# Tap products as two 32-column matmuls in branch order, put back through DRAM; one warm-up token fewer; an earlier operand load

## The reference

```python
# layer 1: graph convolution over joints, then four branches over time
x = concat([x[:, :h], einsum('bctv,vw->bctw', x[:, h:], A_flat)])
x = concat([x[:, :h] @ A_intra, x[:, h:] @ A_inter])
y = relu(bn(conv1x1(x + x @ An, Wgc)))
b1 = bn(tconv(relu(bn(conv1x1(y, Wb1))), Wt1, dilation=1))   # 5 taps over time, 8 channels
b2 = bn(tconv(relu(bn(conv1x1(y, Wb2))), Wt2, dilation=2))   # 5 taps, 8 channels
b3 = bn(maxpool3(relu(bn(conv1x1(y, Wb3)))))
b4 = bn(conv1x1(y, Wb4))
t = relu(concat([b1, b2, b3, b4]) + res)                     # res is the input x
# layer 2: attention over the 400 tokens of each of 32 batches, on the normed t
q, k, v = three projections to 32 channels
scores = exp(-(|q|^2 + |k|^2 - 2 q.k));  t = t + softmax(scores) @ v
# layer 3: norm, projection, batch norm over all tokens, then a recurrence over the tokens
y_t = sigmoid(wx_t + y_(t-1) @ V.T);  out = t + y
```

## Time and profile before

| | |
|---|---|
| median of 3 runs | 237.83 us (237.70 to 238.28) |
| profiled execution | 237.66 us, span 235.8 us, mean TensorE clock 0.956 |
| busy, share of span | PE 199.2 us (85%), PEld 94.1 (40%), DVE 157.7 (67%), ACT 169.9 (72%), POOL 27.5 (12%) |
| DMA | 26.83 MB, mean 114 GB/s, one queue |
| head, first pair | 0 to 30 us |
| loop | 30 to 88 us; VectorE's `add_x` stands at 45.82, 65.46 and 85.10 |
| attention | to 199 us |
| recurrence | 208.9 to 227 us, then the output stores |

### The profile page before, as it was taken

The page is one execution under the profiler, slowest core; times in us unless marked ns, Lnnn a source line. Parts: engine busy times, 40 slices in busy tenths (PEclk is TensorE's granted clock), DMA queues, the critical chain, the costliest instruction groups (busy, mean ns, idle before and its releaser), DMA issues. The chain is left out here.

```text
span 235.8 us, 3561 instructions
## 1 busy us (share of the span) xinstructions
PE 199.2 (85%) x1110; PEld 94.1 (40%) x1110; DVE 157.7 (67%) x296; ACT 169.9 (72%) x309; POOL 27.5 (12%) x44
## 2 busy tenths in 40 slices
PE   0775998898899797959989999999999998588950
PEld 0552554464465353523333343434343333245630
DVE  0417618965992992399578577777869695595880
ACT  4028179579759959797998999999899984365640
POOL 6000000054024006016100101010101000000000
PEclk9997699999999999997999999999999999889985
DMA  6940020039599709348880716162520000000016
GB/s 173 372 126 0 0 72 1 0 77 348 160 273 285 221 0 308 129 138 296 212 215 0 192 23 190 22 169 47 176 37 0 3 0 0 0 3 0 0 51 233
DMA packets 26883, 26.83 MB, mean 114 GB/s; under 512 B 1550, under 2 KB 25806, under 8 KB 26740
## 3 DMA queue, kind: packets, MB, share of 16 engines
q1 hardware_dynamic: 26868, 26.64, 38.6%
HBM read 14.74 MB, written 11.88 MB: 113 GB/s over the span
## 5 line engine op out<-in xcount | busy, mean ns | idle before, releaser
L474 ACT ACTIVATE arena<-ps 128x800 f32<-128x800 f32 (+1 forms) x56 | 44.5, 796 | 6.5 <-PE ps L980 4.9
L481 ACT ACTIVATE arena<-arena 128x800 f32<-128x800 f32 (+1 forms) x56 | 46.3, 829 | 0.0
L980 PE MATMUL ps<-qa,ka 128*128 128x400 bf16 (+1 forms) x128 | 35.8, 343 | 3.6 <-ACT arena L474 3.6
L980 PE MATMUL ps<-qb,kb 96*128 96x400 bf16 (+1 forms) x128 | 35.7, 341 | 0.0
L702 DVE TENSOR_TENSOR psum<-arena 128x400 f32<-128x400 f32 x32 | 19.6, 612 | 13.5 <-ACT arena L481 13.4
L702 DVE TENSOR_TENSOR psum<-psum,arena 128x400 f32<-128x400 f32 x32 | 19.5, 609 | 7.2 <-ACT arena L481 5.8
L1013 PE MATMUL ps<-arena,vb 128*32 128x400 f32 x192 | 21.0, 513 | 0.8 <-issue 0.8
L905 PE MATMUL ps<-arena,cst 128*128 128x400 f32 x32 | 15.7, 620 | 6.5 <-DVE arena L627 6.5
L980 PEld LDWEIGHTS ps<-qa,ka 128*128 128x128 bf16 (+1 forms) x128 | 10.4, 98 | 26.9 <-ACT arena L474 10.0
L1094 PE MATMUL ps<-yb,cst 128*128 128x160 f32 x76 | 17.2, 335 | 2.2 <-ACT yb L551 1.3
L711 DVE RECIPROCAL arena<-ps 128x400 f32<-128x400 f32 x7 | 18.6, 2651 | 0.0
(11 more groups left out here) (137 smaller groups left out, 357.4 us busy)
## 6 DMA issues: line engine op xcount, KB each, us to landing
dka<-arena SPq DMA_DIRECT2D x16, 200.0 KB, 3.1
dqa<-arena SPq DMA_DIRECT2D x16, 200.0 KB, 3.2
ka<-dka SPq DMA_DIRECT2D x8, 400.0 KB
qa<-dqa SPq DMA_DIRECT2D x8, 400.0 KB
arena<-x_tok SPq DMA_DIRECT2D x4, 400.0 KB
t<-x SPq DMA_DIRECT2D x1, 1600.0 KB, 12.1
dkb<-arena SPq DMA_DIRECT2D x8, 200.0 KB, 3.5
dqb<-arena SPq DMA_DIRECT2D x8, 200.0 KB, 4.6
```

The source lines that it names most:

```text
L474: nc.scalar.activation(prob[par][:, lo:hi, :], ps[:, o:o + hi - lo, 0:N], ACT.Exp, scale=2.0).then_inc(e1_done, 1)
L481: nc.scalar.activation(p, p, ACT.Exp).then_inc(p_ready, 1)
L980: last = mm_(ps[row:row + keys, bank, 0:N], kk[par][0:rows, b, o:o + keys], qq[par][0:rows, b, :], start=first, stop=not first, skip_group ...
```

## The change

The parts, in the order of the program:

1. x goes into `t0` in branch order, by 16 transfers of 8 partitions in place of one of 128.
2. GpSimd reorders the columns of an identity, of the middle-tap matrix and of the tap matrices; the two tap matrices shrink to 32 columns each. TensorE makes from them a centering matrix and two columns with scale and shift in branch order, and VectorE copies both out of PSUM (three copies where there was one).
3. `taps` now does the middle product first, over all 128 columns, and then two products of 32 columns, one per branch, into PSUM partitions 0 to 31 and 32 to 63. VectorE's maximum is moved ahead of its copies for the second branch.
4. `t_relu` writes to `outs` (now also `pre_t`), in branch order; `center` reads it there with the reordered matrix. For the residual the tensor is stored to DRAM (`store_t`, one transfer per pair) and loaded into `t0` in the old order (`load_t`, four transfers per pair). `residual` waits for them.
5. SyncE's queue is written out without loops: `load_t` and `store_t` stand ahead of `store`, and the operands of group 2 are loaded ahead of the last `de` store.
6. The first sweep starts at token 1 in place of token 0 (`SKIP`), and the seed blocks are cut differently.

```diff
-BLOCKS = ((0, 1), (1, 4), (4, 7), (7, 10))
+BLOCKS = ((0, 2), (2, 5), (5, 8), (8, 10))
+SKIP = 1
...
+        dt = nc.dram_tensor("dt", [PAIRS, P, 2 * N], F32, kind="Internal").ap()
...
+        pre_t = outs
...
+            def store_t(i):
+
+                sp.wait_ge(t0_ready, 2 * i + 2)
+                sp.dma_start(dt[i], pre_t[:, 2 * i:2 * i + 2, :].rearrange("p g n -> p (g n)")).then_inc(t_stored, 16)
+
+            def load_t(i):
+
+                sp.wait_ge(t_stored, 16 * i + 16)
+                if i:
+                    sp.wait_ge(t_in, 16 * NB * i)
+                for b in range(NB):
+                    sp.dma_start(t0[C * b:C * b + C, 2 * i:2 * i + 2, :].rearrange("p g n -> p (g n)"),
+                                 dt[i].rearrange("(j b r) n -> b j r n", j=BR, b=NB)[b]).then_inc(t_in, 16)
...
-            sp.dma_start(t0[:, :, :], x.rearrange("g p n -> p g n")).then_inc(x_in, 16)
+            for j in range(BR):
+                for b in range(NB):
+                    o, to = C * b + CB * j, C * j + CB * b
+                    sp.dma_start(t0[to:to + CB, :, :],
+                                 x[:, o:o + CB, :].rearrange("g p n -> p g n")).then_inc(x_in, 16)
...
-            store(0)
-            for par in range(2):
-                load_operands(0, par)
-            with sp.Fori(1, PAIRS) as i:
+            def load_next(i, par):
+
+                sp.wait_ge(s_done, UNITS * (2 * i + par - 1))
+                load_operands(i, par)
+
+            for i in range(PAIRS - 1):
+                if i:
+                    load_t(i - 1)
+                store_t(i)
                 store(i)
-            with sp.Fori(1, PAIRS) as i:
-                for par in range(2):
-                    sp.wait_ge(s_done, UNITS * (2 * i + par - 1))
-                    load_operands(i, par)
+                store_e(i)
+                if i == 0:
+                    for par in range(2):
+                        load_operands(0, par)
+            load_t(PAIRS - 2)
+            store_t(PAIRS - 1)
+            store(PAIRS - 1)
+            load_next(1, 0)
+            store_e(PAIRS - 1)
+            load_next(1, 1)
+            load_t(PAIRS - 1)
+            for i in range(2, PAIRS):
+                for par in range(2):
+                    load_next(i, par)
...
+            def order_by_branch(dst, src):
+
+                nc.gpsimd.tensor_copy(dst[:, :].rearrange("p (j b r) -> p j b r", b=NB, j=BR),
+                                      by_branch(src)).then_inc(by_branch_ready, 1)
+
+            order_by_branch(ident_b, c_("ident"))
+            pool.wait_ge(late_in, 16)
+            order_by_branch(middle_b, c_("middle"))
+            for j in range(2):
+                o = COLUMNS["taps"][0] + P * j
+                nc.gpsimd.tensor_copy(taps_b[:, C * j:C * j + C].rearrange("p (b r) -> p b r", b=NB),
+                                      by_branch(cst[:, o:o + P])[:, j]).then_inc(by_branch_ready, 1)
...
-                    nc.scalar.activation(at(t0, g), ts[par], ACT.Relu,
-                                         bias=bn_h2[:, S_POST:S_POST + 1]).then_inc(t0_ready, 1)
+                    nc.scalar.activation(at(pre_t, g), ts[par], ACT.Relu, bias=post[:, 1:2]).then_inc(t0_ready, 1)
...
-                step(h, 0)
-            for s in range(1, L):
+                step(h, SKIP)
+            for s in range(SKIP + 1, L):
                 for h in range(2):
-                    act.wait_ge(pre[h], s)
+                    act.wait_ge(pre[h], s - SKIP)
                     step(h, s)
             act.wait_ge(cmp_c, 1)
-            steps(L)
+            steps(L - SKIP)
...
-                    dve.wait_ge(mx_ready, g + 1)
-                    mid = z[64:96, PAD:PAD + N]
-                    nc.vector.tensor_tensor(mid, mid, mx[par][64:96, :], ALU.max).then_inc(pooled, 1)
+                        if j == 0:
+                            dve.wait_ge(mx_ready, g + 1)
+                            mid = z[64:96, PAD:PAD + N]
+                            nc.vector.tensor_tensor(mid, mid, mx[par][64:96, :], ALU.max).then_inc(pooled, 1)
...
-            dve.wait_ge(x_in, 16)
+            dve.wait_ge(x_in, 16 * BR * NB)
             y_copy(0)
             tap_inputs(0)
             dve.wait_ge(wc_done, 1)
-            nc.vector.tensor_copy(wc[:, :], ps[:, 5, 0:P]).then_inc(wc_ready, 1)
+            nc.vector.tensor_copy(wc[:, :], ps[:, 5, 0:P])
+            nc.vector.tensor_copy(center_b[:, :], ps[:, 6, 0:P])
+            nc.vector.tensor_copy(post, ps[:, 7, 0:2]).then_inc(wc_ready, 1)
+            dve.wait_ge(wc_ready, 1)
...
+                dve.wait_ge(t_in, 16 * NB * (g // 2 + 1))
...
-                    o = COLUMNS["taps"][0]
+                    pe.wait_ge(pooled, 2 * i + par + 1)
+                    mm_(ps[:, 2 * par + 1, 0:N], middle_b[:, :], zp[par][:, PAD:PAD + N],
+                        start=True, stop=False, skip_group_check=True)
+                    pe.wait_ge(u_act, 2 * i + par + 1)
+                    pe.wait_ge(u_ready, 2 * (2 * i + par) + 2)
                     for j in range(2):
-                        pe.wait_ge(u_ready, 2 * (2 * i + par) + j + 1)
-                        if j:
-                            pe.wait_ge(u_act, 2 * i + par + 1)
-                        mm_(ps[:, 2 * par + 1, 0:N], cst[:, o + P * j:o + P * j + P], tap_in[par][j],
-                            start=(j == 0), stop=False)
-                    pe.wait_ge(pooled, 2 * i + par + 1)
-                    mm_(ps[:, 2 * par + 1, 0:N], c_("middle"), zp[par][:, PAD:PAD + N],
-                        start=False, stop=True).then_inc(tapped, 1)
+                        last = mm_(ps[C * j:C * j + C, 2 * par + 1, 0:N], taps_b[:, C * j:C * j + C], tap_in[par][j],
+                                   start=False, stop=True, skip_group_check=True)
+                    last.then_inc(tapped, 1)
...
-            mm_(ps[:, 5, 0:P], c_("center"), c_("wT"), start=True, stop=True).then_inc(wc_done, 1)
+            pe.wait_ge(by_branch_ready, 4)
+            mm_(ps[:, 5, 0:P], c_("center"), c_("wT"), start=True, stop=True)
+            mm_(ps[:, 6, 0:P], ident_b[:, :], c_("center"), start=True, stop=True)
+            mm_(ps[:, 7, 0:2], ident_b[:, :], small[:, 21:25:3], start=True, stop=True).then_inc(wc_done, 1)
```

More of the change, by code:

```diff
@@ L107, in build @@
         wc = sb("wc", [P, P])
+        center_b, middle_b, ident_b = (sb(n, [P, P]) for n in ("center_b", "middle_b", "ident_b"))
+        taps_b = sb("taps_b", [P, 2 * C])
         flag = sb("flag", [1, 1], I32)
@@ L164, in build @@
             col(25, 2), col(27, 2), *(col(n) for n in range(29, 35)))
+        post = col(40, 2)
         S_GC, S_Z, S_POST = 0, 1, 2
         K_AT, Q_AT = (0, 1, 2), (1, 2, 0)
+        t_stored, t_in, by_branch_ready = (sem(n) for n in ("t_stored", "t_in", "by_branch_ready"))
         early_in, late_in, x_tok_in, x_in, one_rows, e_stored, out_done = (
@@ L245, in build, with by_branch @@
         ACT_TAPS = (2, 3)
+        pre_t = outs
+        def by_branch(t):
+            return t.rearrange("p (b j r) -> p j b r", b=NB, j=BR)
         def tap_input(par, j, k):
@@ L571, in _ @@
                 with act.Fori(0, NC - 1) as k:
-                    steps(2 * L + L * k)
+                    steps(2 * L - SKIP + L * k)
         @block.vector
@@ L843, in _ @@
                     for h in range(2):
-                        chain(h, 2 * L + L * k)
+                        chain(h, 2 * L - SKIP + L * k)
                         for n in range(len(BLOCKS)):
@@ L916, in center @@
                     pe.wait_ge(v_ready, g + 1)
-                    mm_(ps[:, 4 + 2 * par, 0:N], c_("center"), at(t0, g), start=True, stop=True).then_inc(centered, 1)
+                    mm_(ps[:, 4 + 2 * par, 0:N], center_b[:, :], at(pre_t, g), start=True, stop=True).then_inc(centered, 1)
             def variance(i):
@@ L1103, in steps @@
                         else:
-                            pe.wait_ge(y_ok[h], L * sweep + s)
+                            pe.wait_ge(y_ok[h], L * sweep - SKIP + s)
                         step(h, s)
-            for s in range(1, L):
+            for s in range(SKIP + 1, L):
                 for h in range(2):
                     pe.wait_ge(seeded[h], block_of(s) + 1)
-                    pe.wait_ge(y_ok[h], s)
+                    pe.wait_ge(y_ok[h], s - SKIP)
                     step(h, s)
```

27 lines of the change are left out of this document (15 added, 12 removed).

## The result

The changed kernel took 254.7 us (median of 250.15, 251.54, 257.86 and 259.0), the kernel before 237.84 beside it: ratio 1.055, interval [1.048, 1.061]. The forecast was 246.7 with a range of 240 to 250.5. The direction was right and the loss nearly twice what I expected. The profiled execution is the shortest of the four, 250.15 us, and the changed kernel's runs lie 9 us apart where those of before lie within 0.6 (in the later sessions the runs of before lie up to 4.6 apart, so differences of 1 us there need many runs).

A forecast was written before the change was run, and what follows sets the result against it. No engine fills the span; four stages run in series, with VectorE pacing the loop's taps. Head +5.7, loop +4.5, loads -0.2 and recurrence -1.0 sum to +9.0 on 237.66 us: 246.7, range 240 to 250.5.

The forecast's parts named there:

- The load of x: Head: 8-partition transfers use the same 8 DMA engines, so x takes 8.3 us instead of 4.1; +4.1, bounds 0 to +4.1.
- The clock in the head: Head: longer TensorE idling halves its clock, slowing mixing and branch passes and two new products; +2.8, bounds +0.4 and +4.2.
- The sign I named: Head: TensorE's clock at half from before VectorE's first copy of mixed tokens.
- Taps in the head: Head: only two side-by-side 32-column products remain behind VectorE's last copy; -1.2.
- Taps in the loop: Loop: VectorE's sum is unchanged and the narrow pair replaces the middle product at the end; 0 per round, bounds -0.2 and +0.1.
- The way through DRAM: Loop, third pair: result's stores and four-engine loads delay part stores 6.1 us, 1.6 covered; +4.5 once, bounds 0 and +5.
- The fourth pair's wait: Loop, fourth pair: ScalarE's 1.17 us wait for a part store can shrink or stay; a further +-1.
- Early load: Third group's loads, issued about 1.1 us earlier, remove ScalarE's 0.21 us idling at that group's first scores; -0.2.
- Recurrence: First sweep: one warm-up step of nine goes; -1.0.
- Full spread: Rival: engines take turns, so x and the way back cost only bandwidth; 237.1 us, chance 0.10.
- Cover holds: Rival: third-pair part stores have more room or the four loads spread, so only the head pays; 242.2 us, chance 0.20.
- Clock low for longer: Rival: the loop's stall idles TensorE some 4 us and its clock falls there too; +2, so 249, chance 0.09.

The follow-up runs named there:

- x_host: Changed kernel with x put in branch order by the host ahead of the launch and loaded by one transfer of 128 partitions: 243.24 us, ratio 1.018.
- x16_small: Kernel before with x loaded by 16 transfers of 8 neighbouring partitions, in the old order: 251.04 us, ratio 1.034.
- x_strided: Kernel before with x loaded by 16 transfers of 8 partitions that lie 16 apart: 249.53 us, ratio 1.042.
- x8_16: Kernel before with x loaded by eight transfers of 16 neighbouring partitions: 246.94 us, ratio 1.039.
- fixed: Changed kernel with x in branch order from the host by one transfer, and the result's stores and loads behind the part stores: 238.95 us, ratio 0.995.
- fixed_full: As fixed, but with the tap products put back to two of 128 columns in the old order: 237.9 us, ratio 0.989.
- best: Kernel before with one warm-up token less, group 2's operands loaded early, and VectorE's wait for x moved to the first add_x: 234.95 us, ratio 0.987.
- skip_only: Kernel before with the first sweep started at token 1 and nothing else changed: 236.73 us, ratio 0.993.
- t_late: Changed kernel, x still by small transfers, with load_t and store_t moved behind each pair's part stores: 251.74 us, ratio 1.054.
- x_wait_late: Changed kernel with VectorE's wait for x moved from the first copy of mixed tokens to the first add_x: 248.2 us, ratio 1.042.
- load_late: As x_host, with only the four loads of t per pair moved behind the part stores, the stores of t staying ahead: 237.67 us, ratio 0.999.
- x16_wide: Kernel before with x loaded by 16 transfers of 128 partitions and half a group each: 238.3 us, ratio 0.999.

## Why the prediction was right or wrong

The forecast summed to +9.0; the profiled run shows +12.5 and the median +16.9. In the profiled run x's load took 1.9 more than its term, the taps 1.0 more in the head and 0.5 in the loop, the recurrence 1.1; the fourth pair and the stall gave back 1.8, and some 0.8 is spread over the rest. What the median has beyond it went with x's load (x_host).

- **"The load of x", +4.1: mechanism right, size wrong.** A DMA share near 0.5 was foreseen and came (0.52 to 0.57). But the engines did not keep their 25 GB/s: 0.54 x 16 = 8.6 busy engines moved 171 GB/s, 20 each. In x16_small it was 9, in x_strided 14. This load cost +5.95 in the shortest run, and by the medians x_host, which loads x whole, is 11.5 us below the changed kernel. The step that failed is the upper bound, "1638 KB at 198 GB/s last 8.3 us": eight engines at the 25 GB/s of the token load. That load writes 100 partitions in one transfer; with 16 per transfer and all engines busy x8_16 shows 148 GB/s, 9 per engine. This is the main error of the forecast. Why narrow transfers are slow is shown only in part, by the spacing of the written partitions. The unevenness is mostly this load's too (x_host's runs lie 1.4 apart), but fixed and fixed_full load x whole and spread over 5.2 and 7.7 us, which no run explains. The Trainium skill's divisor rule (DMA: Bandwidth & Descriptors, "Why a DMA increments its semaphore by 16 and not by 1") agrees with the share; that section says nothing of rates.
- **"The clock in the head", +2.8: +2.4 without x's delay (x_host), +2.9 with it.** The size is right, the reason is not, so this was luck. I had the slow pace come from TensorE's longer idling. It came in x_host after 0.75 us of idling and in best, the old convolution, after none, and stayed away before after 1.24. The sign I named did not show either: the four mixing passes took 3.01 us, but the granted clock reads 1.00 until about 30 us. What sets the pace there stays open.
- **"Taps in the head", -1.2: -0.6 in x_host, -0.2 in the changed kernel.** Half too large or more; against the wide products of fixed_full, at full clock, it is a loss.
- **"Taps in the loop", 0 per round: +0.27**, outside my bound of +0.1. I counted the pair's length and not what TensorE does behind it: the next weights wait for the narrow pair to end. The Trainium skill (TensorEngine Tiling (Array Packing), "Key Properties", "Mode switching requires drain") says that a change between tiling modes lets the array run empty first. The row of L1005, 0.65 us idle, agrees; I had mentioned the drain and given it no time.
- **"The way through DRAM", +4.5 in the third pair: +3.98.** Right in place and nearly in size. The landing moved by 6.4 us in x_host (forecast 6.1), 2.1 for the stores (2.0) and 4.3 for the loads (4.1), with four engines at 25 GB/s in the windows. The cover was mis-sized: about 2.3 us and not 1.6, since 6.4 of delay made 4.1 of stall there (22.60 against 18.48); and I gave SyncE's 2.7 us of issuing the loads no time.
- **The fourth pair's wait** "can shrink or stay": it went, -1.3.
- **Early load, -0.2**: the wait of 0.21 is not separable in time; no run tried this edit alone.
- **Recurrence, -1.0: right in skip_only (18.98 against 19.98) and in the changed kernel's code too (t_late and x_host, -1.0), +0.1 in the profiled run.** The steps before the clock's return took 1.36 each in the changed kernel's profile (4.75 for three and a half); skip_only's first took 1.25, and then 0.99. Why the clock came back late in that run, nothing here shows. No third sweep ran.
- **Rivals.** *Full spread* fell with the first row (20.21 against 14.26). *Cover holds* fell with 3.38 and 1.92 us of waiting. *Clock low for longer* put the low clock behind the stall in the loop; there it read 1.00; only one slice of 40 dips, later, as before.
- **The range** ended at 250.5, because I took "eight engines at full rate" as the worst case of a form that the trace of before does not contain.

## What to carry to other kernels

Reordering partitions by many small transfers is not paid in bytes. Look at how many partitions a transfer writes and how near they lie, and keep one transfer over all 128 where the order can be made elsewhere. A slow transfer also holds back what waits behind it on the same queue (x_wait_late), so moving the wait off the critical engine is not enough. Put transfers that nobody waits for soon behind those that free a buffer: load_late's span is 4.0 us shorter than x_host's by that alone (236.6 against 240.6). A product of a quarter of the columns was not cheaper here, where wide products follow it. And one profile is one execution: the recurrence's gain was missing in one profile and there in two others with the same code.

## What the runs showed of the hardware that I had not expected

- x's load in 16 transfers of 8 partitions moved 171 GB/s in one run at a share of 0.54 and about 75 in another at 0.55, and ended at 20.2, 24.7 or 30.8 us in three profiles of this shape.
- DMA share near 1 does not mean bandwidth: 1.08 and 148 GB/s (16 neighbouring partitions), 1.09 and 224 (8 apart), 1.05 and 390 (one transfer of 128, the kernel before from 10 to 12 us).
- TensorE's first four mixing passes took 3.0 us in x_host, fixed, load_late, fixed_full and best, and 1.58 in before, skip_only and x16_wide, all where the granted clock reads 1.00. The idle time before them was 0.75, 0.95, 1.06, 0.79 and none, against 1.24, 0.90 and 1.54. The passes' own time showed the slow pace; neither the clock record nor the idle time did.
- Loads of 32 partitions ran at a share of 0.25 to 0.26 and 102 GB/s: four engines, 25 GB/s each (changed kernel from 96 us, load_late from 86).
